# A fused attention and expert program: exponentials over two banks at once, and GpSimd's operations between the phases cut up or moved

## Time and profile before

| | us |
|---|---|
| median of 3 runs | 756.27 |
| lowest and highest of them | 750.86 and 763.96 |
| the profiled execution | 754.25 |
| its span, first to last instruction | 752.5 |
| mean granted TensorE clock | 0.943 |

### The profile page before, as it was taken

How to read it: one execution, slowest core, us unless ns; L and a number is a source line. 1 busy time by engine, 2 the same in 40 slices (tenths; PEclk the granted TensorE clock), 3 DMA queues, 4 the chain that set the end, 5 groups by cost and what they waited for, 6 DMA issues and landing times.

```text
span 752.5 us, 11357 instructions
## 1 busy us (share of the span) xinstructions
PE 697.5 (93%) x4038; PEld 481.3 (64%) x4038; DVE 508.3 (68%) x1129; ACT 405.5 (54%) x746; POOL 107.0 (14%) x107
## 2 busy tenths in 40 slices
PE   7999999999999999986899999999999999999675
PEld 5878987898779887884535534555555455455354
DVE  5667457655676556867776787979777985842451
ACT  5674357544664466432155756765556764647322
POOL 0202220222013430350101010100002000000100
PEclk9999999999999999998569999999999999969976
DMA  8300000010000110025305500550005500000000
GB/s 335 141 2 1 29 1 2 1 45 0 0 0 11 35 45 1 4 35 103 70 2 85 86 1 2 85 85 2 2 1 86 113 2 2 2 1 29 30 0 28
DMA packets 13996, 28.30 MB, mean 38 GB/s; under 512 B 2612, under 2 KB 3452, under 8 KB 13820
## 3 DMA queue, kind: packets, MB, share of 16 engines
q1 hardware_dynamic: 13948, 27.68, 15.8%
HBM read 12.60 MB, written 2.10 MB: 20 GB/s over the span
## 4 chain that ended last, share of the span: by engine, by line
PE 71%; DVE 18%; ACT 5%; issue 4%; DMA 2%; POOL 1%; DVEq 0%; ACTq 0%; SPq 0%; POOLq 0%
PE bank_y L414 11%; PE bank_q L355 10%; PE bank_st L1184 8%; DVE nmax L1767 7%; PE bank_c L1197 6%; PE bank_a L298 5%; PE bank_a L385 3%; PE side L1256 3%; PE side L1130 3%; PE side L1287 2%; PE bank_a L332 2%; PE side L1144 2%; PE bank_n L370 2%; PE bank_q L397 2%; PE side L1216 2%
## 5 line engine op out<-in xcount | busy, mean ns | idle before, releaser
L1767 DVE TENSOR_REDUCE nmax<-bank_s 128x1 f32<-128x512 f32 x240 | 154.1, 683 | 56.7 <-PE bank_s L1161 55.5
L1513 ACT ACTIVATE shared<-bank_st 128x512 f32<-128x512 f32 x256 | 139.0, 595 | 69.2 <-PE bank_st L1184 68.3
L1184 PE MATMUL bank_st<-qs,ks 50*128 50x512 f32 x256 | 103.2, 473 | 5.6 <-ACT shared L1513 4.1
L1161 PE MATMUL bank_s<-ks,qs 48*128 48x512 f32 x240 | 101.8, 484 | 4.8 <-DVE nmax L1767 2.2
L617 DVE SCALAR_TENSOR_TENSOR sq<-bank_q,bq,eq 128x512 f32<-128x512 f32 x64 | 47.6, 743 | 48.2 <-ACT eq L500 48.2
L414 PE MATMUL bank_y<-m_hi,s_lo 128*128 128x256 f32 x256 | 73.2, 286 | 3.2 <-POOL s_lo L250 3.1
L1184 PEld LDWEIGHTS bank_st<-qs,ks 50*128 50x128 f32 x256 | 42.0, 194 | 52.8 <-issue 26.1
L1197 PE MATMUL bank_c<-shared,v 128*32 128x512 f32 x512 | 74.1, 653 | 0.9 <-ACT shared L1513 0.9
L414 PE MATMUL bank_y<-m_lo,s_hi 128*128 128x256 f32 x256 | 72.1, 282 | 0.0
L414 PE MATMUL bank_y<-m_hi,s_hi 128*128 128x256 f32 x256 | 72.1, 282 | 0.0
L250 POOL TENSOR_TENSOR s_lo<-sq,s_hi 128x512 fp32r<-128x512 f32 x32 | 42.8, 1338 | 186.1 <-ACT s_hi L505 186.1
(11 more groups left out here) (267 smaller groups left out, 1354.7 us busy)
## 6 DMA issues: line engine op xcount, KB each, us to landing
qs<-qk_hi SPq DMA_DIRECT2D x16, 256.0 KB, 4.8
ks<-qk_hi SPq DMA_DIRECT2D x16, 256.0 KB, 7.2
xT<-in_xT SPq DMA_DIRECT2D x4, 512.0 KB, 4.4
sq<-in_wqT SPq DMA_DIRECT2D x2, 1024.0 KB, 9.3
wo<-in_woT SPq DMA_DIRECT2D x1, 2048.0 KB, 13.3
xs<-in_x SPq DMA_DIRECT2D x1, 2048.0 KB, 18.2
qs<-qk_lo SPq DMA_DIRECT2D x8, 256.0 KB, 5.4
ks<-qk_lo SPq DMA_DIRECT2D x8, 256.0 KB, 7.5
```

Source lines behind the costliest of these rows:

```text
L1161: pe.matmul(score_bank(b, u)[:, :], qs[part, b % 2, slot, t * P:(t + 1) * P], ks[part, b % 2, slot, :], start=True, stop=True).then_inc(s_ ...
L1184: pe.matmul(bank_st[u % 2][:, :], ks[part, b % 2, slot, kt * P:(kt + 1) * P], qs[part, b % 2, slot, :], start=True, stop=True).then_inc(st ...
L1513: act.activation(probs[:, u % SLOTS, :], bank_st[u % 2][:, :], ACT.Exp, scale=SCALE1).then_inc(p_ready, 1)
L1767: dve.tensor_reduce(nmax[:, g, t, j:j + 1], score_bank(b, u)[:, :], AX.X, ALU.max, negate=True).then_inc(max_ready, 1)
```

## The change

The two banks of turned scores become one tensor of two banks. TensorE's matmuls and their waits stay word for word. The exponentials of a pair are one operation of 128x1024 over both banks, which waits for both scores and counts `p_ready` up by two when it ends. Between the phases, GpSimd no longer clears all of v but only columns 17 to 31 of each head, in eight operations (one for each parity and tile), after batch 1's tiles have been normalised; its low part of the experts' weights waits for `split_maxima(0, 0)`; `value(0, 1)` is issued behind head 5 instead of head 2, `turn_hm(1)` behind head 6 instead of 5, and ScalarE's `value_out(0, 1)` behind `shift_out(0, 0)`.

```diff
-        bank_st = [ctx.enter_context(nc.psum_tensor(f"bank_st{i}", [P, 512], F32)) for i in range(2)]
+        both_st = ctx.enter_context(nc.psum_tensor("bank_st", [P, 2, 512], F32))
+        bank_st = [both_st[:, i, :] for i in range(2)]
...
             pool.wait_ge(first.y_done, H0 * B)
-            pool.memset(v[:, :, :, :, :], 0.0).then_inc(zeros_ready, 1)
-            pool.wait_ge(zeros_ready, 1)
+            pool.wait_ge(x1_ready, 2 * NT)
+            for parity in range(2):
+                for t in range(NT):
+                    pool.memset(v[:, parity, t, :, DH1 + 1:], 0.0).then_inc(zeros_ready, 1)
+            pool.wait_ge(zeros_ready, 2 * NT)
             pool.memset(v[:, :, :, :, DH1:DH1 + 1], 1.0).then_inc(v_ones_ready, 1)
             hidden_update(1)
+            pool.wait_ge(nmax_lo_ready, 1)
             split_weights(1, RAW_SPLIT, RAW_END, win_hi, win_lo)
...
-                if h == 2:
-                    value(0, 1)
                 if h == 4:
                     turn_max(0, 0)
                 if h == 5:
+                    value(0, 1)
+                if h == 6:
                     turn_hm(1)
...
             def exponentials(b, s, js):
                 if 0 in js:
                     at_least(act, pv_done, SUBS * b + s - 1)
-                for j in js:
-                    u = 4 * s + j
-                    act.wait_ge(st_done, 64 * b + u + 1)
-                    act.activation(probs[:, u % SLOTS, :], bank_st[u % 2][:, :], ACT.Exp, scale=SCALE1).then_inc(p_ready, 1)
+                u = 4 * s + js[0]
+                act.wait_ge(st_done, 64 * b + u + 2)
+                act.activation(probs[:, u % SLOTS:u % SLOTS + 2, :], both_st[:, :, :], ACT.Exp, scale=SCALE1).then_inc(p_ready, 2)
...
-            value_out(0, 1)
             act.wait_ge(first.y_done, H0 * B)
             split_weights(1, RAW_SPLIT, RAW_END, win_hi)
             shift_out(0, 0)
+            value_out(0, 1)
             hmT_out(1)
```

## The result

The changed kernel takes 766.75 us (median of 4 runs, 764.52 to 769.04), the one before 755.05 beside it: a ratio of 1.0192, with a 95% interval of 1.015 to 1.0235. It is slower by 11.7 us, clear of noise, and just short of the 2% that the prediction takes runs of this kernel to tell apart. The ratios leave out executions over 1.5% above the fastest of their kernel (here one of before, 763.96 us), while the medians and the fit further down keep them; without them (100 runs) the fit's slope is 0.281 and no kernel's difference at equal clock moves by more than 1.3 us. The profiled execution took 769.04 us, span 767.0, mean granted clock 0.924 (before: 754.25, 752.5, 0.943).

What follows compares the result with a forecast made beforehand. TensorE was taken as the bound, busy 93% of the span and 71% of the chain. Terms 0 - 4.0 - 1 + 8.0 = +3.0 us gave 757.3 from the profile or 759.3 from the median; forecast 758, range 743 to 772.

Steps and rivals of the forecast that it cites:

- two of the rivals: Nothing of the joined operation's waits swallowed, 769.6 us, chance 0.18; clock stays up through the opening, 745.9 us, chance 0.15.
- The memset, taken at 0: Between the phases: VectorE is no longer held, but the DMA lands no sooner; 0 us, bounds -1.7 and 0.
- the rival of 0.10: Between the phases: memsets and split hold another VectorE operation and the 1.55 us stay; 759.6 us, chance 0.10.
- Value(0,1) and the split, -4.0: Between the phases: VectorE's idle -3.80, cast stall -1.55, TensorE late +1.35; -4.0 us, bounds -5.35 and -2.45.
- The lower clock after it, -1 with bounds 0 and -7: Opening, 357.5 to 390 us: with TensorE's idle 3.5 us gone, less loss at clock 0.50; -1 us.
- the first rival: Batches: clock falls in the new waits before next pairs; over 2% slower, ten such twos give 775 us; chance 0.12.
- The joined operation, 1.03 us: ScalarE in the batches: one 128x1024 exponential takes 1.03 us, saving some 0.05 a pair, counted as nothing (bound -1).
- The waits, 15.8 at the first matmul and 8.0 at the last: Borders between pairs: TensorE waits for the joined exponential; upper bound 15.8 us, lower 4, taken as 8.0.
- the rule's first-matmul figures: Borders between pairs: delay of the first matmul from when banks come free; 2.6 us late start, 10.5 late release.
- its signs: Batches: longer by more than 16 us, or mean clock under 0.95 in the second and third.
- my "against": Batches: clock was 1.00 in the second and third batch, where TensorE waits as well; weighed against a rival of chance 0.12.

Runs made afterwards that it cites:

- e4: e2 plus 17 added matmuls, results unused, keeping TensorE busy before the first score until the key DMA lands; 750.3 us, ratio 0.9947 to the kernel before.
- e2: Kernel before with only the changes between the phases (memset, split, value(0,1)), exponentials one by one; 754.2 us, ratio 0.9986.
- e3: e2 with GpSimd's old single memset of all v back in its place; 753.2 us, ratio 0.9997 to the kernel before.
- e1: Kernel before with only the joined exponentials, between the phases all as before; 766.5 us, ratio 1.0175.
- e8: Changed kernel plus added matmuls, results unused, in the opening and at the end of batch 0; 758.1 us, ratio 1.007 to the kernel before.
- e5: Kernel before, but both separate exponentials of a pair wait until both turned scores are done; 755.1 us, ratio 0.9993.
- e6: Kernel before, but a pair's first turned score waits until both exponentials of the pair before are done; 757.2 us, ratio 1.0014.
- e9: e2 plus added matmuls in the opening, at batch 0's end and behind heads 2, 3, 4, 6, 7; `res_ready` wait ahead of scores; 749.8 us, ratio 0.9939.

## Why the prediction was right or wrong

The time, 766.75, lies in the range of 743 to 772, which was wide enough for two of the rivals; the forecast of 758, "no change", was 9 us short. What it had wrong is the clock, which it let move in the opening alone and there only to the better. By its steps:

- **The memset, taken at 0.** The DMA landed no sooner, right: first score 12.4 us behind phase one in both traces. But the step looked only at what starts later or earlier and not at what TensorE does meanwhile. Its wait for the DMA grew from 1.58 to 4.67 us and the clock fell some 9 us earlier. My bounds, -1.7 and 0, held no loss. The parts of the memset held nobody, so the rival of 0.10 is out: VectorE's L655 took 1.22 us beside them and 1.21 before, without them.
- **Value(0,1) and the split, -4.0.** The stall went (0.17), the old hole too, and the new one behind head 5 measured 2.21 us for my 1.35 (the middle of 0 and 2.90, which I said I took, is 1.45), with 0.52 more behind head 6. With the clock kept through heads 0 and 1 (e4) the opening was 3.6 us shorter, near the 4.0; without, 0.3. At equal clock over the whole program the fit gives these edits only 1.0 to 1.6 us (e2, e3, e4).
- **The lower clock after it, -1 with bounds 0 and -7.** This is the step that failed, with its sign. The bounds held no loss at all. The opening's edits alone (e2) spend 5 us more at the lower level than before, not less, by the fit 1.5 us of loss (inside the noise of the runs, +- 4 us at the lower level). The whole changed kernel spends 17 us more, by the fit 5.5 us; the larger part of these comes with the joined operation and belongs to the first rival.
- **The joined operation, 1.03 us:** 1.023. That ScalarE gains nothing by it: right, its idle time before exponentials grew from 69.2 to 99.6 us, more than the 8.1 us it saved. The Trainium skill's 1.04 (ScalarE: Activation LUTs, "What ACT_TABLE_LOAD costs") agrees with 1.023.
- **The waits, 15.8 at the first matmul and 8.0 at the last.** TensorE's idle time behind ScalarE grew by 16.0 us in the changed kernel (18.3 in e1), and e1 cost 8.0 (+- 0.9) at equal clock, the changed kernel 7.5 more than e2. Right in both sizes, the second within some 2 us (the stretches compared under e8 give 5.7 for the changed kernel), and e5 and e6 (4.0 and 10.0 for 2.6 and 10.5) roughly bear out the rule's first-matmul figures. That the rule is right pair by pair isn't shown; by batch the cost is uneven, 2.3 us in batch 0 and 0.6 in batch 2.
- **The first rival** (the clock falls in the batches) had 0.12 and was, at a quarter of its 17 us, the rest of the loss: joined kernels have 13 us more at the lower clock, 4.3 us by the fit. e5 and e6 have a part of the waits each and no more time at the lower clock. Of its signs one came (batch 1 at a clock of 0.91, batch 2 at 1.00) and one didn't (the batches grew by 12.7 us together, not 16). The rule of the Trainium skill that I weighed there (TensorE: Matmul & The Clock Gate, "A second HAM failure mode: psum-queue depth-cycling") named the danger, and I gave it too little; the runs agree so far that the kernels with more such waits spend more time at the lower clock (104 against 91 us), and don't show that the waits are why. That one trace can't show it is visible in e2 to e6: their batch 1 also ran 15 to 21 us at the lower clock, with separate exponentials. The profile of before had its usual total (86 us, mean 91) but none of it in batch 1; my "against", drawn from its 1.00 in two batches, was one draw from a wide spread.

The sum again, with what was measured: -1.6 (e2) + 8.0 (e1) = 6.4 at equal clock, where the changed kernel has 6.0, and 5.5 for the clock: 11.5 us, the difference of the means of all runs (the fit makes its two parts add up to that; only 6.4 against 6.0 is a test).

## What to carry to other kernels

Joining two operations over a double buffer saves the second one's start and takes the double buffering away: work out when each half comes free before and after, and count only where nothing else stands between. Measure such a delay at the last thing the receiving group waits for, not at the first; here that halved it, and the total came out. Compare variants at equal time at the lower clock: one profile of each would have put 7 us of this loss into batch 1, where kernels without the change have them too. And when an edit makes TensorE finish sooner in front of a wait that doesn't move, price the longer idle time by what the clock does behind it; a few matmuls whose results nobody uses, in front of a wait of known length, gave 4.4 us here (e4 against e2), and the edits themselves at most 1.6 at equal clock.

## What the runs showed of the hardware that was not expected

The same program spread over 15 us from run to run (standard deviation 4.2, and 1.6 once the mean granted clock is taken out): 0.325 us for each us at 1.2 GHz, where work that TensorE alone bounds would give 0.5 (that the rest is time in which VectorE bounds is my reading; no run shows its share). A memset on GpSimd of 3.6 us held VectorE's normalisations, SBUF to SBUF, until its end, while two maxima read from PSUM took 1.28 us as always within a GpSimd operation of 3 us:

```profile
362.37 1.28 DVE L1767 TENSOR_REDUCE nmax<-bank_st 128x1 f32<-128x512 f32 x2
```

Eight memsets of 240 elements took 1.97 us together, 0.25 each, where one of 128 alone takes 0.32 to 0.36: they took little more than half of the 3.6 us that I estimated. And once the clock had fallen, a full TensorE did not bring it back soon: 14.00 of 14 us busy at 0.50 in e9, and 14.72 of 15 us at 0.50 in the kernel before:

```profile
375.00:390.00 15.00, 14.72 (x48) 6.21 (x48) 10.59 (x26) 5.43 (x10) 0.08 (x1) 0.50 0.01 2
```
